# Block loads and routing tables of a two-layer gated transformer kernel, put in another order

## What is computed

```python
x = x + tanh(g_xattn[1]) * fusion(layernorm(x), ctx)      # softmax(x c^T) c
xt = layernorm(x).reshape(2048, 128)
logits = xt @ Wr + br
pr, idx = top_k(logits, 2)                                # 8 experts, 2 per row
w = softmax(pr)
for e in range(8):
    h = silu(xt @ W1[e] + b1[e]) * (xt @ W2[e] + b2[e])   # 128 -> 512
    y = y + (h @ W3[e] + b3[e]) * cw[:, e:e + 1]          # 512 -> 128
x = x + tanh(g_ffn[1]) * y
```

## Time and profile before

| | |
|---|---|
| median of 3 executions | 630.33 us (629.39 to 630.82) |
| the profiled execution | 636.85 us |
| its span, first to last instruction | 635.0 us |
| mean granted clock of TensorE | 0.941 of full |
| TensorE matmuls busy | 561.3 us, 88% of the span |
| VectorE / ScalarE / GpSimd busy | 412.8 / 320.8 / 206.4 us |
| chain that ended last, by engine | PE 64%, DMA 9%, DVE 8%, SP queue 7%, POOL 4%, issue 4%, ACT 3% |
| all DMAs | 71.19 MB, mean 112 GB/s |

### The profile page before, as it was taken

How to read it: one execution, slowest core, us unless ns; L and a number is a source line. 1 busy time by engine, 2 the same in 40 slices (tenths; PEclk the granted TensorE clock), 3 DMA queues, 4 the chain that set the end, 5 groups by cost and what they waited for, 6 DMA issues and landing times.

```text
span 635.0 us, 9965 instructions
## 1 busy us (share of the span) xinstructions
PE 561.3 (88%) x3295; PEld 331.8 (52%) x3307; DVE 412.8 (65%) x1054; ACT 320.8 (51%) x652; POOL 206.4 (32%) x217
## 2 busy tenths in 40 slices
PE   2776899999998799999999999999786969899991
PEld 1432344444453244444444445545575969899991
DVE  4759968989347599678334566557786656344455
ACT  2535646666656875555454527282544424344440
POOL 4907701010032363001782310001654655233330
PEclk9786969999998999999999999999978889899996
DMA  7376791000039500000012002000005878899965
GB/s 268 101 191 101 181 197 26 3 3 3 2 120 325 191 0 1 1 0 0 0 57 76 0 1 20 0 1 0 29 25 149 291 224 270 280 292 328 311 212 206
DMA packets 48010, 71.19 MB, mean 112 GB/s; under 512 B 11110, under 2 KB 35112, under 8 KB 47672
## 3 DMA queue, kind: packets, MB, share of 16 engines
q1 hardware_dynamic: 44968, 65.61, 35.3%
q0 software_dynamic: 2272, 4.69, 2.0%
q10 hardware_dynamic: 720, 0.27, 0.2%
HBM read 59.18 MB, written 21.29 MB: 127 GB/s over the span
## 4 chain that ended last, share of the span: by engine, by line
PE 64%; DMA 9%; DVE 8%; SPq 7%; POOL 4%; issue 4%; ACT 3%; POOLq 0%; DVEq 0%
PE psum L1953 21%; PE psum L2224 7%; PE psum L1898 5%; PE psum L1755 4%; PE psum L1768 4%; PE psum L2235 4%; POOL sorted_x L792 3%; PE psum L1900 3%; SPq L513 3%; PE psum L1950 2%; PE psum L1776 2%; DMA wb<-in_wall_dram 2%; PE psum L1732 2%; DMA xb<-sorted_x 2%; PE psum L1782 2%
## 5 line engine op out<-in xcount | busy, mean ns | idle before, releaser
L1953 PE MATMUL psum<-hidden,ew 128*128 128x512 f32 x320 | 143.8, 592 | 0.6
L880 ACT ACTIVATE probs<-psum 128x512 f32<-128x512 f32 x128 | 74.6, 598 | 50.0 <-PE psum L1755 49.6
L1953 PEld LDWEIGHTS psum<-hidden,ew 128*128 128x128 f32 x320 | 60.7, 190 | 69.4 <-issue 68.1
L1164 DVE TENSOR_REDUCE negmax<-psum 128x4 f32<-128x1024 f32 x64 | 76.9, 1210 | 19.9 <-PE psum L1732 19.5
L2224 PE MATMUL psum<-xbT,wb 128*128 128x128 f32 x624 | 81.2, 286 | 1.3 <-DMA wb<-in_wall_dram 1.3
L2224 PEld LDWEIGHTS psum<-xbT,wb 128*128 128x128 f32 x624 | 77.5, 202 | 1.8 <-DMA wb<-in_wall_dram 1.7
L1081 ACT ACTIVATE silu_g<-psum,wb 128x128 f32<-128x128 f32 x156 | 44.6, 368 | 66.0 <-PE psum L2224 66.0
L1647 DVE SCALAR_TENSOR_TENSOR gated<-psum,wb,silu_g 128x128 f32<-128x128 f32 x156 | 43.9, 344 | 48.2 <-ACT silu_g L1081 41.6
L817 POOL DMA_INDIRECT sorted_y<-yb,xb x39 | 37.5, 962 | 69.0 <-DVE yb L1639 66.9
L1755 PE MATMUL psum<-stacks 50*128 50x256 bf16 x256 | 51.0, 291 | 5.0 <-DMA stacks<-maxT 2.9
L2235 PE MATMUL psum<-wb,gated 128*128 128x128 f32 x312 | 42.8, 281 | 3.4 <-DVE yb L1639 3.4
(11 more groups left out here) (254 smaller groups left out, 954.6 us busy)
## 6 DMA issues: line engine op xcount, KB each, us to landing
wb<-in_wall_dram SPq DMA_DIRECT2D x39, 516.0 KB, 5.1
wb<-in_wall_dram SPq DMA_DIRECT2D x39, 256.0 KB, 5.0
sorted_x<-in_slots_dram SPq DMA_DIRECT2D x1, 9815.0 KB, 32.6
stacks<-stacked SPq DMA_DIRECT2D x12, 384.0 KB, 8.4
xb<-sorted_x SPq DMA_DIRECT2D x39, 65.0 KB, 3.6
stacked<-parts SPq DMA_DIRECT2D x6, 384.0 KB, 3.4
back<-sorted_y SPq DMA_DIRECT2D x4, 512.0 KB, 5.5
stacked<-parts SPq DMA_DIRECT2D x6, 256.0 KB, 3.3
```

The lines of the kernel that those rows point to most:

```text
L880: nc.scalar.activation(probs[:, g % 2, h % 4, :, :], s2[n % 2].rearrange("p (k q) -> p k q", k=2), ACT.Exp, scale=float(HD) ** -0.5).then_ ...
L1164: nc.vector.tensor_reduce(negmax[:, p].rearrange("p h q -> p (h q)"), psum[:, i:i + 2, :].rearrange("p h (q k) -> p (h q) k", q=2), AX.X, ...
L1953: last = nc.tensor.matmul(dst, ew2[:, j, cols], hidden[:, c, k - 1, j, :], start=False, stop=(j == 3))
```

## The change

In `load_blocks`, the first rows of the middle and late tables are issued ahead of the first weights of the table, and three instead of four of them come first. The loop then issues weights j and rows j + 3 in turn, as before.

On POOL, five instead of six scatters of chunk 0 come before the power of norm 3 of chunk 1, and three instead of two scatters of chunk 2 before the first result of a block. After the results of blocks 0, 1 and 2 come two, two and one of the remaining five (it was two each). Chunk 3's eight scatters go two each behind the results of blocks 3 to 6 (it was one each behind blocks 3 to 10).

On DVE, the table half of the early table moves behind fuse(5), maxima2(7) and third_stats(2). The middle table's halves, both behind block 4's products before, are now behind those of block 4 and of block 5; the late table's, both behind block 8's before, are behind those of block 7 and of block 8. No instruction is added or removed.

```diff
             def load_blocks(first, end, table, rows):
                 sp.wait_ge(table, 1)
-                load_weights(first)
                 sp.wait_ge(rows, 16 * GR)
-                for j in range(first, first + AHEAD + 1):
+                for j in range(first, first + AHEAD):
                     load_rows(j)
-                for j in range(first + 1, end):
+                for j in range(first, end):
                     load_weights(j)
                     if j + AHEAD < end:
                         load_rows(j + AHEAD)
...
             second_weights(0)
-            send_rows(0, range(0, 6))
+            send_rows(0, range(0, 5))
             rstd_of_chunk(3, 1)
-            send_rows(0, range(6, GR))
+            send_rows(0, range(5, GR))
             rstd_of_chunk(2, 2)
...
             second_weights(2)
-            send_rows(2, range(0, 2))
+            send_rows(2, range(0, 3))
...
                 if j < 3:
-                    send_rows(2, range(2 * j + 2, 2 * j + 4))
+                    send_rows(2, range(2 * j + 3, min(2 * j + 5, GR)))
                 if j == 1:
                     second_weights(L)
-                if 3 <= j < 3 + GR:
-                    send_rows(L, range(j - 3, j - 2))
+                if 3 <= j < 7:
+                    send_rows(L, range(2 * j - 6, 2 * j - 4))
...
             fuse(4)
             maxima2(6)
-            table_of_blocks(0, early_table, EARLY, early_ready)
             fuse(5)
             maxima2(7)
             third_stats(2)
+            table_of_blocks(0, early_table, EARLY, early_ready)
             layer_norm_rows(2)
...
                 if j == 4:
                     blocks_of(1)
+                if j == 5:
                     table_of_blocks(1, middle_table, MIDDLE, middle_ready)
+                if j == 7:
+                    blocks_of(2)
                 if j == 8:
-                    blocks_of(2)
                     table_of_blocks(2, late_table, LATE, late_ready)
```

## The result

The kernel after took 629.50 us (median of 20 executions, 623.54 to 652.24); the kernel before, run beside it, 634.38 us (20 executions, 628.37 to 659.16). The ratio is 0.9931 (95%: 0.9903 to 0.9960): **4.4 us or 0.7% faster**, the interval reaching from 2.5 to 6.2 us. The forecast was 7.1 us from 630.33. So the side was right and the time, 629.5, lies above the range, which ended at 627.4.

A forecast was written before the change was run, and what follows sets the result against it. Late blocks were taken as bound by TensorE, with DMA nearly full at 0.95. Gains of 2.0 early, 2.3 middle, 0.3 for the late table's split and 2.5 late sum to 7.1 us: 630.33 becomes 623.2, range 619.3 to 627.4.

The forecast's parts named there:

- part (c): Before the blocks: last early scatter lands sooner with weight 0 behind it, rows leave earlier; 2.0 us, bounds 0 and 2.1.
- my first rival: Before the blocks: the early scatter lands no sooner, its 4.95 us not being weight 0's doing; 625.2 us, chance 0.13.
- My bound of 0 for this part: Before the blocks: no gain if the scatter still lands at 483 to 484, or weight 0 takes 7.0 us.
- Part (d): Middle blocks: yb wait goes, block 9's rows leave earlier but are still awaited 2.6 us; gain 2.3, bounds 0.9 and 4.9.
- my second rival: Middle blocks: TensorE's lower clock behind the wait for block 9's rows goes too; 620.6 us, chance 0.15.
- hidden or 1.4 late: Middle blocks: weight 9, now behind three rows, lands at 522.9, wanted at 521.5 to 525.2 depending on the clock.
- Part (e): Late blocks: block 17's row wait and slow stretch go, 3.3 us by block 17; 2.5 net, bounds 1.4 and 4.7.
- What I charged for the weights behind: Late blocks: 0.8 us off the 3.3, for weights landing late on a shorter lead and DMA with little room.
- the third rival: Late blocks: the stage is bound by the pace of its weights and hands its gain back; 625.7 us, chance 0.12.
- The slower rival: Late blocks: transfers meet, weights land every 3.2 us instead of 2.88, eating all; 632.4 us at 3.3; chance 0.06.

The follow-up runs named there:

- two pairs: The kernels before and after profiled side by side on two chips: the original measurement (ratio 0.9931) and the repeat on the third chip (0.9914 for the kernel after).
- e18: Kernel before with only the new order of block loads, two rows ahead of the first weights, fifth chip; ratio to before 0.9965.
- e17: Kernel after with two instead of three rows ahead of the first middle and late weights, fifth chip; ratio to before 0.9938.
- e15: Kernel after with the early edits undone (six chunk 0 scatters before the power, early table before fuse(5)), fourth chip; ratio to before 0.9977.
- e16: Kernel after, unchanged, run again on the fourth chip; ratio to before 1.0031.
- before: Kernel before the change, in the original measurement; 634.38 us.
- e11: Kernel before, unchanged, run again on the third chip; ratio to before 1.0019.
- after: Kernel after the change, in the original measurement; 629.50 us, ratio to before 0.9931.
- e10: Kernel after, unchanged, run again on the third chip; ratio to before 0.9914.
- e6: Kernel after with two rows ahead of the first middle and late weights, and block 0's rows ahead of its weights, second chip; ratio to before 0.9934.
- first pair: The kernels before and after in the original measurement, 634.38 and 629.50 us; ratio 0.9931.
- second pair: The kernels before and after run again on the third chip; ratios to before 1.0019 and 0.9914.
- e4: Kernel after with the block loads in their old order, so only the POOL and DVE edits, first chip; ratio to before 1.0021.
- e3: Kernel before with only the new order of block loads, three rows ahead, first chip; ratio to before 0.9987.
- e2: Kernel after, unchanged, run again on the first chip; ratio to before 1.0024.
- e14: Kernel before with only the new order of block loads, two rows ahead of the first weights, fourth chip; ratio to before 0.9962.
- e13: Kernel after with two instead of three rows ahead of the first middle and late weights, fourth chip; ratio to before 0.9983.
- e7: Kernel after, unchanged, run again on the second chip; ratio to before 0.9978.
- e8: Kernel before, unchanged, run again on the second chip; ratio to before 0.9986.
- groups 1, 2 and 4: The three sets of four follow-up kernels run on the first, second and fourth chips; ratios to before from 0.9934 to 1.0031.
- e1: Kernel before, unchanged, run again on the first chip; ratio to before 0.9974.
- e9: Kernel after with four instead of three rows ahead of the first middle and late weights, third chip; ratio to before 0.9964.
- e12: Kernel after with the rows of blocks 0 and 1 ahead of weight 0, third chip; ratio to before 0.9994.
- e5: Kernel after with two instead of three rows ahead of the first middle and late weights, second chip; ratio to before 0.9972.

## Why the forecast was right and where it failed

The side and the mechanism of the middle and late blocks were right. Two terms of the sum failed: the base, 630.33, which was 634.38, and the 2.0 us of part (c), of which 0.1 to 0.6 were measured in the two pairs.

**The base.** I put the sum on 630.33, the median of three executions. Over twenty the kernel before had 634.38. That alone is 4.1 us of the 6.3 us between 623.2 and 629.5. By the executions that the ratio uses, the base would have been 630.5 and the time 626.5, inside the range; what stays is the gain, 4.1 to 4.4 us instead of 7.1. Three executions of a kernel whose executions spread from 628 to 659 don't fix a base, and the range should have held that.

**Part (c) failed: "I take 2.0 us for this part".** It came to 0.6 and 0.1 us by block 2 in the two pairs without idle times, to 0.9 from `e18` to `e17` and 1.2 from `e15` to `e16`. What I said of the last early scatter held: with weight 0 leaving beside it, it landed in 4.95 us (`before`) and 4.8 (`e11`), with weight 0 behind it in 2.3 (`after`, `e10`) and 2.5 (`e18`), so my first rival did not happen; and SP no longer waits for it but for the table. Two steps were off. First, the table ended 31.7 us after T0 (478.51), not 30.8 (480.0 less 449.2): the last maxima came 1.6 us earlier, at 474.96, not the 2.6 forecast. So row 0 left 1.2 us earlier than before (34.5 against 35.65 after T0), not 2.05. Second, I let the rows land as fast as before. Before, weight 0 had left 5.2 us ahead of row 0 while SP waited for the scatters, and the row landed in 2.1 us; now it leaves 1.1 us ahead and the row lands in 3.9. The 1.8 us that this costs is more than the 1.2 gained, so block 0 starts 0.6 later. `e6` shows that it is the order: row 0, ahead of weight 0, is not waited for, and row 1, behind it, takes 3.2 us. And where rows are early, TensorE's own work is next: in `e18` row 0 left 3.1 us earlier than before, and TensorE came to it late. The Trainium skill, "DMA: Bandwidth & Descriptors", Queues, rings and completion order, says that each DMA engine consumes the descriptors of one queue in ring order; the 3.9 and 2.1 us agree with it. My bound of 0 for this part held by block 2 (block 0 itself came 0.6 and 0.2 us later); the reasons I gave for that bound were others.

**Part (d), the middle, was right in its mechanism, low at first and too kind later.** The wait for yb went, 1.9 us, as said. The wait for block 9's rows fell to 1.30 us (1.19 in `e10`), not 2.6: nothing stood ahead of them, and they landed in 2.0 us, not the 3.4 I kept from before. And the low clock behind that idle did not come (1.95 us instead of 3.62 for the matmuls), which was my second rival, given 0.15. Together 4.7 us from block 5 to block 8 (3.8 from block 6 in `e10`) where I forecast 2.3 and at most 4.9. Weight 9 I had as "hidden or 1.4 late", hidden at the low clock that I kept; at the full clock it came 1.23 us late, and weight 10, of which I said nothing, 1.87 us. At the full clock TensorE wants them sooner, and three row issues at 1.1 us stand ahead of them. 1.5 us had gone back by block 10, and in `e10` 3.4 us by block 15. With two rows the two waits shrink to 1.9 us (`e17`). Net of all, and without the early 0.6 and 0.1, the middle gave 3.5 and 0.4 us in the two pairs by block 15, against 2.3.

**Part (e), the late blocks, was right in its mechanism.** Forecast: the 2.98 us idle and the slow stretch go, 3.3 us by block 17. Measured: 4.3 us from block 15 to block 17 in the first pair, 3.9 in the second. The weights were not late by 1.3 us at block 17 (0 and 0.4). What I charged for the weights behind, 0.8 us, was nothing in the first pair (8.4 to 8.8) and 2.5 us in the second (4.4 to 1.9). So the third rival, the pace of the weights, came partly true in the second pair and not in the first. A DMA share of 0.99 in the late window (0.97 in `e10`) leaves little room to refill, but why it went one way here and the other there was not found.

**The slower rival** (weights every 3.2 us) did not happen: 25 matmuls and their loads still take some 2.86 us a block (57 us for 499 matmuls of the late window, 25 a block). On three chips the change was worth nothing that could be measured; what went with that is told below.

**Who carries it.** By the traces, SP's order: without it rows hold TensorE at least as long as before (`e4`), and alone it has 165.6 us to block 38 where the whole has 168.0 (`e3`, `e2`), 163.0 where the whole has 165.9 (`e14`, `e13`) and 158.8 where the whole has 156.6 (`e18`, `e17`). By the timed ratios it is not shown: none of the ratios of halves and wholes on one chip are clear of each other, and `e4` ran on a chip on which the whole change gained nothing either. I had given it half.

Timed, the change is worth 0.7% and 0.9% in two of its five comparisons, and 0.6% with two rows in a sixth; in the other three of the five it can't be told from nothing. The profiled executions say little on its size: from T0 to block 38 the kernel after was 8.8, 0.9 and 1.9 us shorter and once 3.1 longer (`e7`, `e8`) than the kernel before beside it.

## What to carry to other kernels

When a small load and a large one leave on one queue back to back, the small one's landing time is not that of its solitary record: take it from a row in which it has the same neighbour, and ask whose turn it is to be late when it goes first. A wait that is removed lets the engine behind it arrive earlier at all that follows, at full clock earlier still, so cost the next two or three transfers by the new times, not one. A part that comes earlier gains only up to the next bound: at block 0 the rows, weight 0 and TensorE's own work lay within two microseconds of each other. And take the base of a forecast of a per cent from enough executions, or forecast the difference and put the spread of the base into the range.

## What the runs showed that was not expected

**Idle time of ScalarE with nothing to wait for.** On three of the chips (groups 1, 2 and 4) all twelve profiles, of either kernel, have single gaps of 2 to 8 us on ScalarE between blocks 0 and 10 that the trace puts down to "remote" or "issue" and to no engine or DMA. The "remote" part from block 0 to block 38 added up to 6.4 and 7.7 us in the kernel before (`e1`, `e8`), to 15.7, 10.1 and 17.8 in the kernel after (`e2`, `e7`, `e16`), and to 8.4 to 19.8 in the seven others. On the other two chips and in the first pair (`before`, `after`, `e9` to `e12`, `e17`, `e18`) it is zero, and of "issue" there is one of 1.5 us (`e10`). The largest gap, in `e2`:

```profile
505.12 1.14 ACT L1080 ACTIVATE silu_g<-psum,wb 128x128 f32<-128x128 f32 x4 [7.79 <-remote]
```

It is not ScalarE alone that stands. In `e2`, `e4`, `e5`, `e13` and `e16` TensorE stops among the 16 first matmuls of block 4, for up to 1.05 us at a time, put down to "issue" too; no profile without ScalarE's gaps has that.

The results of the kernel after split the same way: the kernel after had 0.9931 and 0.9914 where there were no such gaps, and 1.0024, 0.9978 and 1.0031 where there were. The fastest execution of the kernel before was 628.4, 626.5 and 627.8 us without them, 633.2, 633.9 and 633.4 with them. SP's three row issues took 4.85 us (`e2`), 5.25 (`e7`) and 3.74 (`e16`) there instead of 2.6, which makes the weights behind them later still. That the gaps eat the gain is a reading of this coincidence, not an experiment: I did not find a way to make or remove them. What causes them stays open, and so does whether the change makes them longer: all ten profiles with any part of it have more of them than the two without, but two are few.

**TensorE's clock ahead of T0.** T0 lay between 445.7 and 469.8 us, whatever was changed behind it, and went with the time TensorE had spent at the lower of its two clock levels before: 30.7 or 34.1 us in the profiles with T0 at 445.7 to 447.0, 85.3 us in the two at 466.8 and 469.8. A spread of 24 us is about that of the timed executions, so it goes far to say why twelve of them give an interval of half a per cent, and why a change behind that stage is better read from a mark like T0.
